# Turning half of the combination's low weights by DMA transposes, and splitting the low part of the slot embeddings

## The chip, the cores and the metric

The kernel runs on 1 core of a Trainium2 chip. The time is device microseconds (us) of one execution. Engines are named as in the profile: PE is TensorE (PEld its weight loads), DVE is VectorE, ACT is ScalarE, POOL is GpSimd, SP is SyncE, which here only issues DMAs. A name with a q (SPq, DVEq) is that engine's sequencer. A line number such as L2032 is a line of the kernel before.

## The reference, cut to what matters

A gated delta-rule attention layer, then a soft mixture of experts on its output. x is (4, 2048, 256) in float32.

```python
x = x + attn(layernorm(x))       # scan over 2048 tokens with a 128x128 state for each of 4 batches
xn = rms_norm(layernorm(x), gamma_x)
se = rms_norm(slot_embeds, gamma_slot)               # 8 x 128 = 1024 slots of 256
logits = einsum('bsd,etd->bset', xn, se)             # 2048 tokens x 1024 slots
dispatch = softmax(logits, axis=1)                   # over the tokens
slots = einsum('bsd,bset->betd', xn, dispatch)
processed = gelu(slots @ w1) @ w2                    # hidden width 1024
combine = softmax(logits over all slots, axis=-1)    # over the 1024 slots
x = x + einsum('bnd,bsn->bsd', processed, combine)   # the combination
```

## The kernel before

**The two parts.** `attention` works on chunks of 128 tokens of all four batches at once. Every engine runs the same software pipeline: `step(i, q)` for i from -4 to 15, in which an engine does its share for chunks i to i + 4. The order inside a step is written out by hand for each engine and the engines meet only through semaphores. `moe` then works through the four batches one after the other. A batch has logits and column maxima, dispatch (the slots' inputs), the expert layers (`hidden`, `processed`) for two halves of the slots, and at last the combination.

**High and low parts.** Products that need more than float16 are made of float16 pairs: a value's high part is its rounding to float16, its low part the rounded rest. A product then takes three matmuls: high by high, high by low, low by high.

**The combination.** A batch has 16 tiles of 128 tokens, written as (k, t) with k and t from 0 to 3. For each tile ACT takes the exponential of a row of L in place (`weights`, L1840, 128x1024). DVE casts it to the high part Wh (L1683) and subtracts to get the low part Wl (L1686), in `split_weights`. Both must be transposed, since the matmul contracts over the slots. Wh goes through a DMA transpose into Th that SP issues in `turn` (L1508). Wl is transposed on PE by eight 128x128 transposes into PSUM (`turn`, L2032), and ACT copies the result to Tl (`low_turned`, L1846). PE then makes 24 matmuls of 257 columns into PSUM (`combine`, L2047), and DVE divides by the last column and adds the residual (`finish`, L1745 and L1749). POOL issues the loads of the residual x1t (L1555) and the stores of the result (L1565).

PE's order in the combination is `turn(0,0)`, `processed(1)`, `turn(0,1)`, then for every tile `combine(k,t)` and `turn` of the tile two ahead. DVE's order is `finish(k,t)`, `split_weights(k+1,t)`. SP's order is `turn` tile by tile, in one queue. So each tile's weights are prepared four tiles before they are used, and there are four buffers of Wh, Wl and Th, but two of Tl and of the PSUM tile that the transposes write.

**The slots.** In `attention`, while the pipeline runs, the slot embeddings are scaled: DVE makes the row gxs = 16 gamma_x gamma_slot once (L707), and `slots_scaled` multiplies each of the 8 blocks of 128 slots by its norm's inverse and by gxs (L729), four blocks at each of two places of step -2. ACT makes the high part sp_h in step 0. `slots_low` makes the low part sp_l in one DVE instruction of 128x2048 (L736) in step 1, between the doubling n = 0 and `low_part`. PE transposes both in step 13 (`turn_slots`, which waits for `slots_ok` to be 3).

**DVE's step** in `attention` is, in order: 15 pairs of `product` (L611) and `column` (L622), which depend on each other one after the other, with other short work let in between at fixed counts s; `statistics_in` (L542), `residual` (L670), `moments_in` (L555), `decays` (L579), `system` (which writes M, L597), `doubling` 0 (L636), `low_part` (which writes Xl, L701), `statistics` (L680), `turned_low` (L563), `right_side` (L644), `doubling` 1 (L636), and the rest. PE's second `turn_Z` (L1169) and all that stands behind it in PE's order waits for doubling 0, its third for doubling 1.

## Time and profile before

| | |
|---|---|
| Time, median of 3 runs | 1182.07 us (1180.25 to 1182.2) |
| The profiled execution: its time | 1181.81 us |
| its span | 1180.2 us |
| mean granted clock of PE | 0.978 of full |
| PE busy | 1117.5 us, 95% |
| DVE busy | 944.2 us, 80% |
| ACT busy | 736.9 us, 62% |
| POOL busy | 322.9 us, 27% |
| DMA traffic | 93.97 MB, mean 80 GB/s |

The time is some 1.6 us longer than the span, which is what lies before the first and after the last instruction of the trace. A busy share is an average over stages with different limits, so what a change in one stage is worth has to be read from that stage.

### The profile page before, as it was taken

The page shows a single profiled execution, that of the slowest core. Times are in us where ns is not written, and L with a number is a line of the kernel's source. Part 1 is how long each engine was busy: PE and PEld are TensorE (multiplying, and loading weights), DVE is VectorE, ACT ScalarE, POOL GpSimd, SP SyncE. Part 2 cuts the span into 40 slices and gives each one's busy share as a digit, 9 for nine tenths or more (in the row PEclk, how much of TensorE's full clock was granted, in tenths as well). Part 3 has the DMA queues.
Part 4 walks back from the last instruction along what each step waited for, and adds up shares of the span by engine and source line. Part 5 has one row for each costly group of instructions (what it writes and reads, how often), then busy time and mean ns, then how long its engine had stood idle before and what let it go on. Part 6 is the DMA issues. An engine that isn't in the chain of part 4 may idle for free.

```text
span 1180.2 us, 26880 instructions
## 1 busy us (share of the span) xinstructions
PE 1117.5 (95%) x8600; PEld 860.1 (73%) x8600; DVE 944.2 (80%) x2193; ACT 736.9 (62%) x1386; POOL 322.9 (27%) x391
## 2 busy tenths in 40 slices
PE   4599899999999979999999999999999999999998
PEld 2487788888888765487786486787486787487787
DVE  5888888888888856998586998576998666998665
ACT  4446556666676545597663697674597764497763
POOL 3847555667556621000022000022000022000022
PEclk9699999999999988999999999999999999999999
DMA  6113322333323252331274031364030355000165
GB/s 198 49 45 99 117 78 83 89 89 114 109 80 89 82 129 67 99 73 45 63 157 95 2 72 36 72 137 114 2 72 27 72 129 129 1 2 1 19 125 126
DMA packets 185512, 93.97 MB, mean 80 GB/s; under 512 B 123680, under 2 KB 176928, under 8 KB 185440
## 3 DMA queue, kind: packets, MB, share of 16 engines
q1 hardware_dynamic: 178384, 75.40, 26.9%
q0 software_dynamic: 5792, 17.05, 5.0%
q8 instruction: 49, 0.80, 0.3%
q10 hardware_dynamic: 1264, 0.53, 0.2%
q14 instruction: 23, 0.19, 0.1%
HBM read 38.42 MB, written 29.36 MB: 57 GB/s over the span
## 4 chain that ended last, share of the span: by engine, by line
PE 71%; DVE 13%; issue 7%; ACT 3%; POOL 0%; DMA 0%; DVEq 0%; ACTq 0%; SPq 0%; POOLq 0%
PE m_wide L2047 14%; PE m_wide L1927 11%; PE m_wide L2021 7%; PE m_wide L2007 7%; PE a_bank L1118 4%; DVE m_Dm L1627 3%; PE a_bank L1130 3%; DVE m_El L1635 2%; PE m_wide L2032 2%; ACT m_Eh L1810 2%; PE a_bank L1180 2%; PE a_bank L1256 2%; PE a_bank L1169 2%; PE m_wide L1981 2%; PE a_bank L1220 1%
## 5 line engine op out<-in xcount | busy, mean ns | idle before, releaser
L1565 POOL DMA_DIRECT2D out_dram<-m_o x64 | 35.4, 553 | 620.9 <-DVE m_o L1749 508.9
L1981 PE MATMUL m_wide<-m_X,m_Eh 128*128 128x257 f16 (+1 forms) x1024 | 171.0, 273 | 2.1 <-DVE m_El L1635 1.6
L1927 PE MATMUL m_wide<-seT,XT 128*128 128x512 f16 x672 | 147.7, 380 | 1.0 <-issue 1.0
L2047 PE MATMUL m_wide<-m_Ph,m_Th 128*128 128x257 f16 x512 | 140.5, 274 | 0.0
L1981 PE MATMUL m_wide<-m_X,m_El 128*128 128x257 f16 (+1 forms) x512 | 139.8, 273 | 0.0
L2047 PE MATMUL m_wide<-m_Ph,m_Tl 128*128 128x257 f16 x512 | 139.5, 273 | 0.0
L2047 PE MATMUL m_wide<-m_Pl,m_Th 128*128 128x257 f16 x512 | 139.2, 272 | 0.0
L1927 PEld LDWEIGHTS m_wide<-seT,XT 128*128 (+1 forms) x672 | 65.7, 98 | 78.9 <-issue 2.0
L1981 PEld LDWEIGHTS m_wide<-m_X,m_Eh 128*128 128x128 f16 x1024 | 99.3, 98 | 18.9 <-issue 3.1
L1783 ACT COPY L<-m_wide 128x512 f32<-128x512 f32 (+1 forms) x112 | 65.1, 584 | 74.6 <-PE m_wide L1927 73.8
L1803 ACT ACTIVATE m_E<-m_Dm,m_eshift 128x512 f32<-128x512 f32 x128 | 92.5, 722 | 21.1 <-DVE m_Dm L1627 20.6
L1846 ACT COPY m_Tl<-m_wide 128x1024 f16<-128x1024 f16 x64 | 64.6, 1010 | 61.6 <-PE m_wide L2032 61.6
L1635 DVE TENSOR_TENSOR m_El<-m_E,m_Eh 128x512 f16<-128x512 f32 x128 | 87.8, 689 | 7.4 <-ACT m_Eh L1810 3.3
L1627 DVE TENSOR_TENSOR m_Dm<-L,m_Mb 128x512 f32<-128x512 f32 x128 | 87.7, 685 | 0.0
L2021 PE MATMUL m_wide<-w2s,m_hh 128*128 128x256 f16 x512 | 84.5, 273 | 0.0
L1598 DVE TENSOR_TENSOR cmax<-cmax,L 128x512 f32<-128x512 f32 x112 | 77.2, 689 | 8.0 <-ACT L L1783 6.6
L2007 PE MATMUL m_wide<-m_sTh,w1s 128*128 128x512 f16 x256 | 77.5, 379 | 0.0
L1810 ACT CAST m_Eh<-m_E 128x512 f16<-128x512 f32 x128 | 77.0, 604 | 0.0
L1604 DVE TENSOR_REDUCE rmax<-L 128x1 f32<-128x512 f32 (+1 forms) x112 | 76.1, 679 | 0.0
L1840 ACT ACTIVATE L<-L,m_nrm (+1 forms) x64 | 73.7, 1152 | 0.9 <-DVE m_nrm L1669 0.9
L2021 PE MATMUL m_wide<-w2s,m_hl 128*128 128x256 f16 x256 | 69.8, 273 | 0.0
L1660 DVE TENSOR_TENSOR m_hl<-m_E,m_hh 128x512 f16<-128x512 f32 x64 | 43.9, 692 | 24.6 <-ACT m_hh L1831 24.5
(199 smaller groups left out, 2739.9 us busy)
## 6 DMA issues: line engine op xcount, KB each, us to landing
L<-in_L_attn_x_dram SPq DMA_DIRECT2D x16, 512.0 KB, 6.8
Mrep<-M_dram SPq DMA_DIRECT2D x32, 256.0 KB
x_dram<-x SPq DMA_DIRECT2D x16, 512.0 KB, 6.3
m_X<-X_dram SPq DMA_DIRECT2D x128, 64.0 KB, 1.8
m_x1t<-x_dram POOLq DMA_DIRECT2D x32, 256.0 KB, 3.6
out_dram<-m_o POOLq DMA_DIRECT2D x64, 128.0 KB, 2.4
M_dram<-M_ SPq DMA_DIRECT2D x16, 256.0 KB, 2.6
X_dram<-Xh SPq DMA_DIRECT2D x16, 256.0 KB, 2.3
```

What stands on the lines that cost most here:

```text
L1598: dve.tensor_tensor(cmax[:, half_at], cmax[:, half_at], L[:, z, bass.ds(tile, 1), :] .rearrange("q a n -> q (a n)"), ALU.max).then_inc(cm_ ...
L1604: dve.tensor_reduce(rmax[:, bass.ds(z * NT + tile, 1)], L[:, z, bass.ds(tile, 1), :] .rearrange("q a n -> q (a n)"), AX.X, ALU.max, negate ...
L1627: dve.tensor_tensor(Dm[p][:, :], L[:, v, bass.ds(4 * g + t, 1), :] .rearrange("q a n -> q (a n)"), Mb[:, v * HS:(v + 1) * HS], ALU.subtrac ...
L1635: dve.tensor_tensor(El[t % 4][:, :], E[t % 4][:, :], Eh[t % 4][:, :], ALU.subtract)\
L1803: act.activation(E[t % 4][:, :], Dm[p][:, :], ACT.Exp, bias=eshift[:, 0:1]).then_inc(E_ok[p], 1)
L1810: act.copy(Eh[t % 4][:, :], E[t % 4][:, :]).then_inc(Eh_ok[p], 1)
L1840: act.activation(row, row, ACT.Exp, bias=nrm[:, bass.ds(4 * k + t, 1)]).then_inc(Ec_ok, 1)
L1927: last = pe.matmul(lg[t % 4], XT[:, sx * KD + k, bass.ds((4 * g + t) * P, P)], seT[:, ss, k, z * HS:(z + 1) * HS], start=(c == 0), stop=(c ...
L1981: last = pe.matmul(acc[v][q], e[t % 4][:, qs], X[:, sx, bass.ds(4 * g + t, 1), 0:XW].rearrange("q a n -> q (a n)"), start=first and e is E ...
L2007: last = pe.matmul(up[f % 2], w1s[:, sw, k, f * P:(f + 1) * P], sT[ss][:, k, :], start=(c == 0), stop=(c == 3 * KD - 1))
L2021: last = pe.matmul(down[q % 2], hT[sh][:, f, q * P:(q + 1) * P], w2s[:, sw, f, :], start=(c == 0), stop=(c == 3 * NF - 1))
L2047: last = pe.matmul(co[p], a, pp[:, e, 0:XW], start=(c == 0), stop=(c == 3 * NS - 1))
```

## The change

1. **Combination.** For tiles with odd t, the low part Wl is transposed by a DMA as well. SP's `turn` gets a second transpose of the same size right behind the first, into Tl_odd, which lies in the room of sTl (for t = 1) and sTh (for t = 3). Since these hold the slots' transposes that `hidden` reads, the first of them in a batch wait on SP for the first of `processed(1)`. PE's `turn` and ACT's `low_turned` are left out for odd t, and PE's and DVE's waits are changed to fit. PE's order is now `combine(k,0)`, `turn(k,2)`, `combine(k,1)`, `combine(k,2)`, `turn(k+1,0)`, `combine(k,3)`.
2. **Low part.** `slots_low` is cut into two instructions of half the size, and these stand between the `product` and `column` pairs, behind s = 3, the first in step 1 and the second in step 12.
3. **Scale row.** gxs is no longer in SBUF but in PSUM, in bank 2.

```diff
-        gxs = sb("gxs", [P, D])
+        gxs = bank[2][:, 0:D]
...
-            def slots_low():
+            def slots_low(first, past):
                 dve.wait_ge(slots_ok, 2)
-                dve.tensor_tensor(sp_l[:, :, :], slots_g[:, :, :], sp_h[:, :, :], ALU.subtract).then_inc(slots_ok, 1)
+                last = dve.tensor_tensor(sp_l[:, first:past, :], slots_g[:, first:past, :], sp_h[:, first:past, :],
+                                         ALU.subtract)
+                if past == NS:
+                    last.then_inc(slots_ok, 1)
...
+                    if s == 3:
+                        if at == 1:
+                            slots_low(0, NS // 2)
+                        if at == NCH - 4:
+                            slots_low(NS // 2, NS)
...
-                if at == 1:
-                    slots_low()
...
+        Tl_odd = [v[:, :, :].rearrange("q k n -> q (k n)").rearrange("q (e n) -> q e n", e=NS) for v in (sTl, sTh)]
...
                 sp.dma_start_transpose(Th[t][:, :, :], Wh[t]).then_inc(T_in[t], 16)
+                if t % 2 == 1:
+                    if isinstance(k, int):
+                        hidden_done = value(sp, (2 * b + 1) * (QS // 2) + 1)
+                        sp.wait_ge(pc, 1)
+                        sp.wait_ge(dn_ps[0], hidden_done)
+                        sp.sem_inc(turning, 1)
+                    sp.wait_ge(Wl_ok, m)
+                    sp.sem_inc(turning, 1)
+                    sp.dma_start_transpose(Tl_odd[t // 2], Wl[t][:, :]).then_inc(T_in[t], 16)
...
-                    dve.wait_ge(T_in[t], 16 * m)
+                    dve.wait_ge(T_in[t], 16 * m if t % 2 == 0 else 32 * m - 16)
...
-                    dve.wait_ge(tp_ps[t % 2], b * HB + 2 * k + t // 2 + 1)
+                    if t % 2 == 0:
+                        dve.wait_ge(tp_ps[t % 2], turned_before(b, k, t) + 2)
...
-                low_turned(0, 1)
                 with act.Fori(0, QB - 1) as k:
                     for t in range(4):
                         weights(k + 1, t)
-                        low_turned(k + (t + 2) // 4, (t + 2) % 4)
-                for t in range(2, 4):
-                    low_turned(QB - 1, t)
+                        if t % 2 == 0:
+                            low_turned(k + (t + 2) // 4, (t + 2) % 4)
+                low_turned(QB - 1, 2)
...
-                    pe.wait_ge(Tl_ok[p], n + 1)
-                    pe.wait_ge(T_in[t], 16 * (b * QB + k + 2))
+                    if t % 2 == 0:
+                        pe.wait_ge(Tl_ok[p], turned(b, k, t) + 1)
+                        pe.wait_ge(T_in[t], 16 * (b * QB + k + 2))
+                    else:
+                        pe.wait_ge(T_in[t], 32 * (b * QB + k) + 48)
...
-                        for a, pp in ((Th[t][:, e, :], Ph), (Th[t][:, e, :], Pl), (Tl[p][:, es], Ph)):
+                        for a, pp in ((Th[t][:, e, :], Ph), (Th[t][:, e, :], Pl),
+                                      (Tl[p][:, es] if t % 2 == 0 else Tl_odd[t // 2][:, e, :], Ph)):
...
                 processed(1)
-                turn(0, 1)
                 cut_to = value(pe, nb * QS + 1)
                 with pe.Fori(0, QB - 1) as k:
                     for t in range(4):
                         combine(k, t)
-                        turn(k + (t + 2) // 4, (t + 2) % 4)
+                        if t % 2 == 0:
+                            turn(k + (t + 2) // 4, (t + 2) % 4)
                 for t in range(4):
                     combine(QB - 1, t)
-                    if t < 2:
-                        turn(QB - 1, t + 2)
+                    if t == 0:
+                        turn(QB - 1, 2)
```

## Rows read from the trace of the kernel before

**Rows 1.** The chain that ended last, first batch's combination: start us, us, what

```profile
576.16 10.48 PE m_wide L2021 x96
586.64 0.45 PE m_wide L2032 x8
587.09 2.65 PE m_wide L2047 x24
...
630.46 5.30 PE m_wide L2047 x48
```

**Rows 2.** Groups by line: count | busy us, mean ns | idle before, releaser

```profile
L1846 ACT COPY m_Tl<-m_wide 128x1024 f16<-128x1024 f16 x64 | 64.6, 1010 | 61.6 <-PE m_wide L2032 61.6
L2032 PE MATMUL m_wide<-ident,m_Wl 128*128 128x128 f16 x512 | 39.0, 219 | 0.0
```

**Rows 3.** Timeline of DVE in the combination: start us, us, instruction

```profile
592.87 0.17 DVE L1745 RECIPROCAL m_cden<-m_wide 128x1 f32<-128x1 f32 x1
...
594.19 1.23 DVE L1686 TENSOR_TENSOR m_Wl<-L,m_Eh 128x1024 f16<-128x1024 f16 x1
```

**Rows 4.** The line that issues SP's transposes: ns min/median/max, and landing

```profile
L1508 SPq DMA_TRANSPOSE m_Th<-m_El x32: 1232/1238/1439, 580.3 to 1165.4; - x32
...
DMA to landing us min/median/max: 3.0/3.5/5.2
```

**Rows 5.** Timeline of SP's queue: the first two transposes of a batch

```profile
569.98 2.83 SPq L1508 DMA_TRANSPOSE m_Th<-m_Eh  x2
```

**Rows 6.** DMA queues in the combination, 590 to 630: packets, MB, engine share

```profile
q1 hardware_dynamic: 12672, 3.15, 50.9%
q0 software_dynamic: 1007, 3.01, 26.3%
```

**Rows 7.** Windows: length, busy PE PEld DVE ACT POOL (x count), PEclk, DMA share, GB/s

```profile
508.00:510.00 2.00, 2.00 (x21) 1.78 (x19) 1.91 (x4) 1.85 (x4) 0.00 (x0) 1.00 1.28 290
...
581.00:582.00 1.00, 1.00 (x11) 0.89 (x10) 0.75 (x2) 0.37 (x1) 0.00 (x0) 1.00 0.48 99
582.00:583.00 1.00, 1.00 (x12) 0.90 (x10) 0.96 (x3) 0.00 (x0) 0.00 (x0) 1.00 0.88 164
```

**Rows 8.** Timeline of DVE's system (M), one each step of attention

```profile
133.93 0.69 DVE L597 TENSOR_TENSOR M_<-a_bank,gamb_ 128x512 f32<-128x512 f32 x1 [0.64 <-DVE gamb_ L579]
...
165.17 0.69 DVE L597 TENSOR_TENSOR M_<-a_bank,gamb_ 128x512 f32<-128x512 f32 x1 [0.66 <-PE a_bank L1160]
...
214.04 0.69 DVE L597 TENSOR_TENSOR M_<-a_bank,gamb_ 128x512 f32<-128x512 f32 x1 [0.59 <-PE a_bank L1160]
...
358.56 0.69 DVE L597 TENSOR_TENSOR M_<-a_bank,gamb_ 128x512 f32<-128x512 f32 x1 [0.61 <-PE a_bank L1160]
```

**Rows 9.** Timeline of step 1, where the low part stands now

```profile
136.14 2.44 DVE L736 TENSOR_TENSOR L<-L 128x2048 f16<-128x2048 f32 x1
...
138.51 2.28 DVE L701 TENSOR_TENSOR Xl<-xf,Xh 128x1024 f16<-128x1024 f32 x1
...
143.02 1.12 PE L1169 MATMUL a_bank<-a_const,Z_ 128*128 128x128 f32 x4 [3.08 <-DVE Z_ L636]
```

**Rows 10.** Windows of step 1, columns as in rows 7

```profile
145.00:147.00 2.00, 2.00 (x13) 1.36 (x12) 0.43 (x1) 0.40 (x2) 0.00 (x0) 0.50 0.67 232
```

**Rows 11.** Timeline of step 1's columns: a bias on DVE, then PE's queries

```profile
123.35 0.42 DVE L570 SCALAR_TENSOR_TENSOR L<-a_bank,bkv 128x258 f32<-128x258 f32 x1
...
124.17 0.38 PE L1130 MATMUL a_bank<-L,wqg_h 128*128 128x512 f16 x1
```

**Rows 12.** Timeline of step -2 and the scaled slots' line: ns min/median/max

```profile
59.29 0.41 DVE L636 TENSOR_TENSOR Z_<-Z_,a_bank 128x256 f32<-128x256 f32 x1
...
63.97 1.05 PE L1193 MATMUL a_bank<-Z_,P1T 128*128 128x64 f32 x8
...
66.06 0.41 DVE L636 TENSOR_TENSOR Z_<-Z_,a_bank 128x256 f32<-128x256 f32 x1
...
L729 DVE SCALAR_TENSOR_TENSOR L<-XT,srn,gxs x8: 454/1476/1744, 55.4 to 63.5; 128x256 f32<-128x256 f32 x8
```

More of the change, by code:

```diff
@@ L1481, in moe, with turned, turned_before @@
         T_in = [sem(f"T_in{u}") for u in range(4)]
+        def turned(b, k, t):
+            return b * HB + 2 * k + t // 2 + 1
+        def turned_before(b, k, t):
+            return turned(b, k, t) - 2
         @block.sync
@@ L1843, in low_turned @@
                     p, n = t % 2, b * HB + 2 * k + t // 2 + 1
-                    act.wait_ge(tp_ps[p], n + 2)
+                    act.wait_ge(tp_ps[p], turned(b, k, t) + 2)
                     act.wait_ge(co_ps[p], n + 1)
@@ L1965, in batch @@
                         for p in range(2):
-                            pe.wait_ge(Tl_ok[p], HB * b + 1)
+                            if p == 0:
+                                pe.wait_ge(Tl_ok[p], HB * b + 1)
                         turn_maxima(0)
@@ L2026, in turn @@
                 def turn(k, t):
-                    p, n = t % 2, b * HB + 2 * k + t // 2 + 1
+                    p = t % 2
                     pe.wait_ge(Wl_ok, b * NT + 4 * k + t + 1)
-                    pe.wait_ge(Tl_ok[p], n)
+                    pe.wait_ge(Tl_ok[p], turned(b, k, t))
                     for e in range(NS):
```

## The prediction

> **What bounds the kernel now.** I read the shares first: PE is busy 95% of the span, but that is a mean over stages, so I went on to the chain that ended last, stage by stage. In the combination it is PE alone: eight transposes (0.45 us), 24 matmuls (2.65 us), again and again with nothing between [rows 1]. A tile costs 3.10 us, and no other engine's time shows. So there a piece of PE's work taken away shortens the kernel by its whole length, until something else becomes the slowest. In attention PE and DVE take turns on the chain. I measured that stage by the distance between two instructions of one kind, one a step [rows 8]: from 214.04 to 358.56 are six steps of 24.09 us, but the one from 133.93 to 165.17 took 31.24. The reader is to see two things: a stage with one bound, and one step of sixteen that is 7.15 us longer than its like. The change touches both.
>
> **The transposes taken from PE.** Of 16 `turn` in a batch 8 go, 32 in the kernel, each 0.45 us on the chain [rows 1]: 14.4 us less. Rows 2 bear out the count: 512 transposes, eight for each of 64 tiles. With them go 32 of ACT's copies of 1.01 us [rows 2], which cost nothing now, as ACT sat waiting for PE before them, and give nothing. The mean tile is then 2.65 + 0.45/2 = 2.875 us, four tiles 11.5.
>
> **Does DVE keep up?** From a tile's reciprocal to the end of its low part are 2.55 us when they run back to back (592.87 to 595.42) [rows 3], below 2.875. The new wait of DVE for the second transpose is for a buffer used four tiles before. No cost, but the cover shrinks from 0.55 to 0.33 us a tile.
>
> **Does SP keep up?** A transpose takes SP 1.24 us [rows 4], and two in a row 2.83 with the waits between [rows 5], so 1.6 us each. Three for each two tiles are 4.8 of 5.75 us. It fits. Behind the new wait for Wl on SP stands the next tile's transpose of Wh. After `combine(k,t)` ends, DVE has Wh some 1.7 us and Wl some 3.1 us later. Wh's landing, 3.5 us from issue [rows 4], has room. For an odd tile: ready at 3.1, landed at 6.6 to 6.8, needed when `combine(k+1,t)` starts, which is 11.5 - 2.65 = 8.85 us after. That leaves about 2 us of slack. At a batch's start the first Tl_odd waits for the first quarter of `processed(1)`, which runs from 576.16 in four equal parts [rows 1], so till 578.8. It lands about 582.4, and the second combination starts after 589: hidden. The wait holds up SP's transpose for tile 2, whose Wh comes later than that anyway.
>
> **Do the DMA engines keep up?** This is the doubtful term. In the combination q1 (the transposes) holds them 50.9% of 40 us for 3.15 MB, which is 12.0 tiles of 0.262 MB, so 1.70 us each; q0 (x1t and results) 26.3%, which over 12.9 tiles is 0.81 us a tile [rows 6]. The new need is 1.5 x 1.70 + 0.81 = 3.36 us a tile, more than 2.875. But a transpose alone takes 0.48 + 0.88 = 1.36 [rows 7], since under load the packets of the two queues stretch each other, and then the need is 1.5 x 1.36 + 0.81 = 2.85. And the share is no hard ceiling at 1: it stood at 1.28 in a window of XT's transposes [rows 7], by which 3.36 would need only 2.63 us. Bounds of the cost: below nothing, as the need is 2.63 to 2.85; above, (3.36 - 2.875) x 12 tiles (the first four of a batch are turned before it starts) = 5.8 us less the 2 us of slack, 3.8 a batch, 15 in all. A gain is excluded. I take 1.5 us in all, near the low end, since two of the three readings lie under 2.875.
>
> By the Trainium skill (DMA: Bandwidth & Descriptors, Issuing engines are not separate DMA queues) DMAs issued from different engines run on the same 16 engines and interleave, which speaks against this change: SP's third transpose takes its time from POOL's loads and stores. The stretch from 1.36 to 1.70 agrees. The same page (Latency and other measured facts) gives 261 GB/s for a transposing DMA in an unfavourable layout; by that 0.262 MB would take an estimated 1.0 us and the need would be 2.3, no stall at all. The trace has 1.36, and goes first.
>
> **The low part leaves its place in step 1.** There one instruction of 2.44 us stands ahead of `low_part`, and that takes 2.28 [rows 9]. PE's third `turn_Z` sits idle 3.08 us for DVE [rows 9], and then PE runs at a granted clock of 0.50, the 1.2 GHz level, at 145 to 147 [rows 10]. So step 1 pays three times: the instruction, the stretched `low_part` behind it, and slow matmuls. With it gone the step should be like its neighbours: 7.15 us less. The two steps after it, (214.04 - 165.17)/2 = 24.44 each [rows 8], should also come to 24.09: 0.7 less. Bounds: 2.44, if the clock falls anyway, to 7.85.
>
> **Its halves in the columns.** Each is half the size, 1.22 us, in a chain that DVE runs without gaps. Behind it on DVE stand two biases; PE's queries wait for the second. That ended at 123.77 and they started at 124.17 [rows 11], so a shift of 1.22 delays PE by 0.8. DVE's own end of step has about 0.64 us of idle time before M [rows 8], so it needs no more. Two halves (step 12 is alike): 1.6 us more, bounds 0 and 2.4. The clock is safe here: PE is in dense matmuls at the time, and a gap of 0.8 is far from 3.08. `turn_slots` in step 13 finds the second half done a step before.
>
> **The scale row in PSUM.** The eight scalings took 1476 ns in the median, but one took 454 [rows 12], so most were held up and not working. In the second group of four the doubling waits behind them: it began at 66.06, and PE's product for it was there at 63.97 + 1.05 = 65.02 [rows 12], so 1.04 us are lost there. For the first group, whose doubling came at 59.29, I add 0.6 as an estimate: PE's other work hides the rest. 1.7 us less. Bounds: nothing, if they stay held up, and 8 x (1.476 - 0.454) = 8.2, if all of it counted; the rows at the doubling are nearer.
>
> By the Trainium skill (SBUF — State Buffer, the section on the shared port pair) a DVE instruction with two SBUF inputs and a GpSimd one that reads SBUF take one port pair in turns, each for its whole length. By that rule a PSUM row ends the hold-up, and the scalings fall to about 0.45 each; without it they stay at 1.48 and this term is 0. The row's spread of 454 to 1744 ns agrees with the rule, which names the cause that I assume.
>
> **Sum.** -14.4 + 1.5 - 7.15 - 0.7 + 1.6 - 1.7 = -20.85. The profiled execution took 1181.81, so 1161.0. The median of the runs is 0.3 higher, so the new median may be too; I say 1161.
>
> **The rivals.**
> 1. The DMA engines become the bound of the combination. For it: the need of 3.36 by the loaded rows. Against: the other two readings, and that a batch's stage is only 12 tiles long with 2 us of slack. It gives between 1163 and 1161 - 1.5 + 15 = 1174.5; half the price is 1167.
> 2. The clock or the stretch stays in attention: the halves open a new gap, or step 1 gives back its 2.44 us alone. Then 7.85 - 2.44 = 5.4 us are missing: 1166.4. For it: PE's other stalls in steps 12 to 15. Against: only step 1 shows the low clock.
> 3. Slower than before, by one loop: the landing of the second transpose. A tile's loop is combine 2.65, DVE 3.1, then the time L from Wl to landing; it must fit in four tiles. Without stalls the sum is -22.35; spread over 48 looped tiles that is 0.47 each, so the kernel is slower once a tile takes over 3.34, that is once L is over 4 x 3.34 - 5.75 = 7.6 us. With L = 8: 3.44 a tile, +27, so 1186.5. For it: the transpose queues behind that of Wh, and four other transfers. Against: landing is 3.5 in the median and at most 5.2 [rows 4].
> 4. The change does little in attention but works in the combination, because the steps' excess has another cause: 1161 + 7.85 + 1.7 = 1170.5. The idle time in rows 9 speaks against it.
>
> **Chances.** Forecast (1158 to 1164) 0.60; rival 1 0.18; rival 2 0.11; rival 4 0.05; rival 3 0.04; within 0.2% of before, by a loaded queue whose price just eats the gain, 0.02. From 1157 to 1173 all but rival 3, that sliver and the far end of rival 1 are held. 0.2%, 2.4 us, is about what a measurement of this kernel can tell from no change. So faster 0.94, same 0.02, slower 0.04.
>
> **What would show it.** In the combination's chain: 2.65 twice for each 0.45, and no wait of PE before L2047; if rival 1 holds, L2047 waits for a DMA, and the first tiles of a batch are clean while later ones are not. The landing of L1508 should rise above 3.5 but stay under 5.5. M in step 1: about 25 us after the one before, granted clock 1.00 throughout; step 12 about 0.8 longer than now. The scalings at about 0.45 us. What would make me wrong: a new stall of PE in `combine`, a low clock in any step, or a DVE that no longer catches up because results land late.

## The result and the profile after

The kernel with the change takes 1162.84 us in the median of four runs (1161.44 to 1165.45), the kernel before 1181.49 beside it. The ratio is 0.9846, with an interval of 0.9826 to 0.9866: 18.7 us faster, where 20.9 were forecast. A second set of five runs on another chip gave 1162.43 against 1182.72, ratio 0.9832 (0.9819 to 0.9845), which is 20.3 us. The execution that was profiled first took 1165.45 (span 1163.8), the slowest of its four. A second profile was taken in the second set, of an execution of 1162.43. The first has the larger stalls, and both are read below.

The page of the kernel after: the busy shares, and from the costliest groups the combination's matmuls and ACT's copies.

```profile
PE 1098.5 (94%) x8344; PEld 841.1 (72%) x8344; DVE 936.2 (80%) x2194; ACT 705.2 (61%) x1354; POOL 321.5 (28%) x391
...
L2076 PE MATMUL m_wide<-m_Ph,m_Th 128*128 128x257 f16 x512 | 141.3, 276 | 6.1 <-DMA m_sTh<-m_Wl 6.0
...
L1871 ACT COPY m_Tl<-m_wide 128x1024 f16<-128x1024 f16 x32 | 32.4, 1013 | 69.7 <-PE m_wide L2057 69.7
```

PE's busy time fell by 19.0 us, from 1117.5 to 1098.5, which is more than the 14.4 of the 32 turns; the rest is in the main matmuls that no longer run at half clock in step 1, where PE is busy 23.8 us instead of 27.9. The copies are 32 instead of the 64 of [rows 2]. The group of `combine` (L2047 before, L2076 now) has a new kind of idle time: 6.0 us, ended by the DMA that writes m_sTh from Wl. It is the only new wait of PE.

**The combination.** The chain of the first batch, to be laid beside [rows 1]:

```profile
575.97 2.65 PE m_wide L2076 x24
578.62 0.45 PE m_wide L2057 x8
579.06 5.30 PE m_wide L2076 x48
...
607.36 0.45 PE m_wide L2057 x8
607.81 2.67 PE m_wide L2076 x24
...
611.88 1.24 SPq L1523
...
613.23 6.30 DMA m_sTh<-m_Wl
...
619.58 2.82 PE m_wide L2076 x24
622.41 17.70 PE m_wide L1951 x82
```

Two tiles, one turn, again and again: 5.75 us for two tiles, as forecast. At the batch's end the chain leaves PE and passes through DVE and SP to a transpose of Wl that took 6.30 us to land. From the first matmul of `processed(1)` (565.49) to the logits of the next batch (622.41) are 56.92 us. Before, the same distance was 59.60 to 59.63 in each of the four batches. The eight turns that went take 3.56 of that (8 x 0.445, the length of a turn in the chain), which would leave 56.04. So the batch stalled for 0.88 us. The four batches took 56.92, 61.27, 57.73 and 57.28, 233.2 in all instead of 238.4: 14.3 us of work are gone, and 9.1 came back as stalls. In the second profile they took 56.98, 56.77, 56.85 and 56.95, 227.6 in all, with 3.4 us of stalls. The worst batch of the first profile, in its chain:

```profile
783.65 1.28 SPq L1523
...
785.08 1.89 SPq L1532
...
787.42 2.61 SPq L1523
...
790.36 1.25 SPq L1523
...
791.73 7.94 DMA m_sTh<-m_Wl
...
799.72 4.48 PE m_wide L2076 x24
804.20 20.72 PE m_wide L1951 x96
```

Three things are longer here than they were before: SP needs 2.61 and 1.89 us to issue a transpose that took it 1.24 in the kernel before [rows 4], the landing takes 7.94 us, and the tile behind the wait takes 4.48 instead of 2.65. SP's queue is part of this path: from 783.65 on it issues one after the other, with no wait for data between. The tile before the last one in the loop of its buffer ended at 788.0, and the last low part was issued 3.7 us after that, where it was 2.76 in the first batch. So of the stall some 1 us came from SP's queue and 1.6 from the longer landing; 0.7 were there in the first batch already. The only wait of PE in the middle of a batch, at 967 in the third, looks alike: there SP took 2.82 us for one issue. Windows of the same place:

```profile
797.00:800.00 3.00, 0.28 (x3) 0.26 (x4) 0.47 (x1) 0.00 (x0) 0.00 (x0) 1.00 0.33 57
800.00:804.00 4.00, 4.00 (x24) 2.92 (x22) 0.01 (x1) 0.00 (x0) 0.54 (x1) 0.57 0.09 33
```

PE sat idle for 3.26 us, and then its granted clock was 0.57 in the mean over 4 us, so some 3.4 of them were at the 1.2 GHz level. The stall of 3.3 us cost 5.2.

**Attention.** The timeline of DVE's M, one a step, with the low part's first half and two of `low_part`, to be laid beside [rows 8, 9]. Step 1 is counted from its M at 131.43 to the next:

```profile
106.71 0.69 DVE L597 TENSOR_TENSOR M_<-a_bank,gamb_ 128x512 f32<-128x512 f32 x1 [1.88 <-issue]
...
118.33 1.22 DVE L736 TENSOR_TENSOR L<-L 128x1024 f16<-128x1024 f32 x1
131.43 0.69 DVE L597 TENSOR_TENSOR M_<-a_bank,gamb_ 128x512 f32<-128x512 f32 x1 [0.60 <-DVE gamb_ L579]
...
133.65 1.42 DVE L701 TENSOR_TENSOR Xl<-xf,Xh 128x1024 f16<-128x1024 f32 x1
...
155.55 0.69 DVE L597 TENSOR_TENSOR M_<-a_bank,gamb_ 128x512 f32<-128x512 f32 x1 [0.67 <-PE a_bank L1166]
...
157.76 2.29 DVE L701 TENSOR_TENSOR Xl<-xf,Xh 128x1024 f16<-128x1024 f32 x1
```

Step 1 takes 155.55 - 131.43 = 24.12 us instead of 31.24, and the granted clock is 1.00 in every window of it. The step before it holds the half in its columns: 24.72 where it took 23.81. The other steps are what they were: 24.64 for the next, then 23.98. Step 12 grew by 0.93. The step that scales the slots fell from 30.12 to 27.3 (28.06 in the second profile). These four differences add up to -7.12 + 0.91 + 0.93 - 2.8 = -8.1 us. The scalings in the timeline of step -2:

```profile
54.84 1.62 DVE L729 SCALAR_TENSOR_TENSOR L<-XT,srn,a_bank 128x256 f32<-128x256 f32 x4
57.74 1.63 DVE L729 SCALAR_TENSOR_TENSOR L<-XT,srn,a_bank 128x256 f32<-128x256 f32 x4
```

Four take 1.62 us. A single one takes 0.47 in the median, where [rows 12] had 1.48.

### The profile page after: what moved, and what is told of

The parts are those of the page before. It is cut to its first block, busy times and chain, and to the rows that moved or that the text cites. A ratio compares the mean times of both kernels' runs of the same rounds, so it can differ in the third digit from the quotient of the medians.

```text
span 1163.8 us, 26301 instructions
## 1 busy us (share of the span) xinstructions
PE 1098.5 (94%) x8344; PEld 841.1 (72%) x8344; DVE 936.2 (80%) x2194; ACT 705.2 (61%) x1354; POOL 321.5 (28%) x391
## 4 chain that ended last, share of the span: by engine, by line
PE 70%; DVE 10%; issue 8%; DMA 4%; ACT 3%; POOL 3%; SPq 2%; DVEq 0%; POOLq 0%; ACTq 0%
PE m_wide L1951 11%; PE m_wide L2076 10%; PE m_wide L2046 7%; PE m_wide L2032 7%; PE m_wide L2006 5%; PE a_bank L1124 4%; PE a_bank L1136 3%; PE a_bank L1186 3%; DMA m_sTh<-m_Wl 3%; DVE m_Dm L1651 2%; PE a_bank L1175 2%; PE a_bank L1262 2%; DVE m_El L1659 2%; ACT m_Eh L1835 2%; PE a_bank L1199 2%
## 5 line engine op out<-in xcount | busy, mean ns | idle before, releaser
L2076 PE MATMUL m_wide<-m_Ph,m_Th 128*128 128x257 f16 x512 | 141.3, 276 | 6.1 <-DMA m_sTh<-m_Wl 6.0
L2076 PE MATMUL m_wide<-m_Pl,m_Th 128*128 128x257 f16 x512 | 139.9, 273 | 0.0
L2006 PEld LDWEIGHTS m_wide<-m_X,m_Eh 128*128 128x128 f16 x1024 | 99.4, 98 | 18.7 <-issue 3.5
L1871 ACT COPY m_Tl<-m_wide 128x1024 f16<-128x1024 f16 x32 | 32.4, 1013 | 69.7 <-PE m_wide L2057 69.7
L1865 ACT ACTIVATE L<-L,m_nrm (+1 forms) x64 | 71.3, 1146 | 0.9 <-DVE m_nrm L1693 0.9
L2076 PE MATMUL m_wide<-m_Ph,m_Tl 128*128 128x257 f16 x256 | 69.7, 272 | 0.0
```

Source lines behind the costliest of these rows:

```text
L1865: act.activation(row, row, ACT.Exp, bias=nrm[:, bass.ds(4 * k + t, 1)]).then_inc(Ec_ok, 1)
L2006: last = pe.matmul(acc[v][q], e[t % 4][:, qs], X[:, sx, bass.ds(4 * g + t, 1), 0:XW].rearrange("q a n -> q (a n)"), start=first and e is E ...
L2076: last = pe.matmul(co[p], a, pp[:, e, 0:XW], start=(c == 0), stop=(c == 3 * NS - 1))
```

## The experiments

Where nothing else is said, a diff is against the kernel with the change.

### Each half of the change alone

The combination alone puts the scale row and `slots_low` back:

```diff
-        gxs = bank[2][:, 0:D]
+        gxs = sb("gxs", [P, D])
...
-                        if at == 1:
-                            slots_low(0, NS // 2)
-                        if at == NCH - 4:
-                            slots_low(NS // 2, NS)
...
+                if at == 1:
+                    slots_low()
```

> The combination part alone, attention as before. Theory A (the 14.4 us of transposes are saved, but in each batch the landing of the last odd tiles is late because the 16 DMA engines are full; some 6 us are lost again): 8 us less than before, 1173.5. Rival B (the two parts need each other, so that the combination alone gives little): under 4 us less, above 1177.5. If the loss were a trait of the profiled run alone: 14 us less, 1167.5.

Measured: 1172.16 against 1182.73, ratio 0.9914 (0.99 to 0.9927), 10.6 us faster. That lies between the 8 of theory A and the 14 of a change without stalls. The four batches took 56.89, 56.88, 57.76 and 56.28: 3.7 us of stalls, where theory A had 6.

This run shows one thing more. Its low part stands in the old place, as it does in the kernel before and in the kernel with the scale row alone. PE's idle time in step 1 is the same in the three profiles, 3.08 to 3.09 us, but what follows differs. Here:

```profile
144.68 1.12 PE L1169 MATMUL a_bank<-a_const,Z_ 128*128 128x128 f32 x4 [3.08 <-DVE Z_ L636]
...
147.00:149.00 2.00, 2.00 (x18) 1.60 (x18) 0.49 (x2) 0.37 (x1) 0.00 (x0) 0.73 0.61 209
```

In the kernel before the clock stays low for longer:

```profile
149.00:151.00 2.00, 2.00 (x11) 1.70 (x10) 1.69 (x8) 0.00 (x0) 0.88 (x3) 0.50 0.00 0
```

Windows of half a microsecond give 3.4 us at the low level here, 6.8 with the scale row alone and 10.2 before, and step 1 takes 28.63, 30.06 and 31.24 us. So each 3.4 us of low clock lengthen the step by 1.2 to 1.4. Carried on to no low clock at all, that is some 27.3 us, an estimate.

Attention alone, as its diff against the kernel before:

```diff
-        gxs = sb("gxs", [P, D])
+        gxs = bank[2][:, 0:D]
...
-            def slots_low():
+            def slots_low(first, past):
...
+                        if at == 1:
+                            slots_low(0, NS // 2)
+                        if at == NCH - 4:
+                            slots_low(NS // 2, NS)
...
-                if at == 1:
-                    slots_low()
```

> The low part in halves and the scale row in PSUM alone, combination as before. Theory A (step 1 loses its 7.1 us, the scalings 2.8, the halves cost 0.9 each, the rest of attention follows): 10 us less, 1171.5. Rival B (the gain before the combination is partly chance of the profiled run): 6 us less, 1175.5. With e1 the two should add up to the whole change, 18.65.

Measured: 1173.2 against 1182.73, ratio 0.9922 (0.9908 to 0.9935), 9.5 us faster. Theory A had said 10. The steps are those of the whole change (24.12 for step 1), and the batches' stages are 59.6 again. The parts add up to 20.1 us, as the whole does in its second set (20.3): within the scatter the two halves don't touch each other.

### Is it the number of transposes?

Only tiles with t = 1 have their low part turned by DMA. Tiles with t = 3 go back to PE. The rest of the diff fits waits and counts to it.

```diff
...
-                if t % 2 == 1:
+                if t == 1:
...
-                        if t % 2 == 0:
+                        if (t + 2) % 4 != 1:
                             turn(k + (t + 2) // 4, (t + 2) % 4)
...
```

> The change, but only tiles with t = 1 go by the DMA transpose, those with t = 3 are turned on PE again. Theory A (DMA engines): the need falls to between 1.25 x 1.36 + 0.81 = 2.5 and 1.25 x 1.70 + 0.81 = 2.9 us a tile, against a tile of 2.99, so no stall: of the 14.4 us 7.2 are left and nothing is lost again, so 1181.5 - 7.2 - 10.5 = 1163.8, about the same as the full change. Rival B (any second transpose in a row makes tiles late): a stall of 2 to 3 us, 1166 or more. Landing of the transposes at most 5.5 us by A.

Measured: 1166.52 against 1182.73, ratio 0.9869 (0.9854 to 0.9884), 16.2 us faster. The stages are 57.81, three times, and 57.85, 231.3 in all. That is 7.1 under the kernel before, what the 16 turns take (16 x 0.445), with no stall. By its total alone the run would have spoken for the rival (1166 or more). But theory A's 1163.8 had counted 10.5 us for attention, which alone gave 9.5, and a kernel before of 1181.5, which was 1182.73 here; 1182.73 - 7.1 - 9.5 = 1166.1. The low parts landed in 4.6 us in the median and 5.5 at most, as A had said. The end of its first batch, in the chain:

```profile
616.74 0.45 PE m_wide L2059 x8
617.19 2.65 PE m_wide L2078 x24
619.84 0.45 PE m_wide L2059 x8
620.28 5.30 PE m_wide L2078 x48
625.59 14.46 PE m_wide L1954 x67
```

So five transposes for four tiles come in time, and six don't quite. The second step down, from t = 1 to t = 1 and 3, brought 3.7 us of its 7 by the medians and the second profile; in the first profile, with 9.1 us of stalls, the stages were 1.9 longer than here.

### POOL's transfers, or SP's queue?

A late transpose can be late because POOL's loads and stores take the DMA engines, or because SP's queue has three to issue. This kernel leaves SP's queue as it is, with all its transposes, and lets POOL's transfers move 16 rows instead of 128 or 256, so most of the output is not written.

```diff
...
-                pool.dma_start(x1t[u][:, :, :], x1_dram[bass.ds(b, 1), bass.ds(at, 2 * P), :]
-                               .rearrange("b (p q) d -> q (b p) d", p=2)).then_inc(x1_in[u], 16)
+                pool.dma_start(x1t[u][0:16, 0, :], x1_dram[bass.ds(b, 1), bass.ds(at, 16), :]
+                               .rearrange("b q d -> (b q) d")).then_inc(x1_in[u], 16)
...
-                               .rearrange("b q d -> (b q) d"), o[p][:, :]).then_inc(o_out[p], 16)
+                               .rearrange("b q d -> (b q) d"), o[p][0:16, :]).then_inc(o_out[p], 16)
```

> The change, but in the combination the residual's loads and the results' stores move only 16 rows of 128 (a sixteenth to an eighth of the bytes), so most of the output is not written and half of the residual not read. SP's queue and all waits are as they are. Theory A (the DMA engines are shared between the transposes and these transfers): no stall, PE never waits for a transpose in the combination, landing at most 4.5 us, 1156.5, six under the change. Rival B (SP's own queue, three transposes for each two tiles in order, is what makes them late): the stalls stay, 1162.

The stages are 56.03, 56.02, 56.03 and 56.06: every stall is gone. The landing of the low transposes, first in the kernel with the change, then here:

```profile
L1532 SPq DMA_TRANSPOSE m_sTl<-m_Wl x16: 1232/1610/2822, 568.3 to 1144.5; - x16
...
DMA to landing us min/median/max: 3.0/5.0/7.9
```

```profile
L1532 SPq DMA_TRANSPOSE m_sTl<-m_Wl x16: 1232/1292/1858, 573.9 to 1142.7; - x16
...
DMA to landing us min/median/max: 3.1/3.4/4.8
```

Three transposes for two tiles are no load that SP can't issue or that the DMA engines can't carry. What makes them late are POOL's transfers. The longest landing, 4.8 us, is a little over the 4.5 expected. That the lateness comes from the engines that both use, and not from the memory behind them, this run doesn't separate; for it speak the shares of the two queues, which add up to more than 1 (below).

The time of this kernel missed the 1156.5 expected of it by 11 us: 1167.92 (ratio 0.9872, 0.9857 to 0.9887). Two causes are seen in its trace, and neither lies in the combination. The stage between attention and the first batch's experts was 171.3 us long, against 167.2 and 168.4 in the two profiles of the kernel with the change, and behind the landing of the last store lie some 7 us in which the trace shows nothing:

```profile
1156.92 0.48 DVE L1776 SCALAR_TENSOR_TENSOR m_o<-m_wide,m_cden,m_x1t 128x256 f32<-128x256 f32 x1
1158.12 0.49 POOL L1591 DMA_DIRECT2D out_dram<-m_o  x1 [2.25 <-DVE m_o L1776]
```

The span is 1167.1, and the store landed 1.7 us after its issue. What the last 7 us are stays open. The stages answer the question of this experiment, the total doesn't.

### The last tile of a batch

In the second profile of the change PE waits once in each batch, for 0.6 to 0.8 us, and each time at the last tile, (3, 3). In the first profile four of five waits stand there. If that one alone is too tight, turning it on PE should take the stall away for one turn a batch. Waits and counts are again fitted to it.

```diff
...
-                if t % 2 == 1:
+                if t % 2 == 1 and not (last and t == 3):
...
-                    if t == 0:
-                        turn(QB - 1, 2)
+                    if t < 2:
+                        turn(QB - 1, t + 2)
...
```

> The change, but the last tile of each batch is turned on PE again. Theory A (the backlog of the DMA engines grows through a batch and is paid at its last tile): four times 0.45 us more for PE, and the stall at the last tile goes, so each combination takes 56.04 + 0.45 = 56.5; 3 us less than the change. Rival B (the stall only moves to the odd tile before, or to the stores): no gain, or 1 to 2 us more.

Measured: 1159.88 against 1182.72, ratio 0.9812 (0.9799 to 0.9825), 22.8 us faster. The kernel with the change had 1162.43 on the same chip. The stages are 56.47, 56.47, 57.31 and 56.5; the work without stalls is 56.04 + 0.445 = 56.48. Three batches have no stall, and the third waited once, for an odd tile with t = 1. The sum of the stages, 226.75, is 0.8 below that of the second profile of the change, which is what this edit is shown to bring; the other 1.7 of the difference of the medians are not in the combination. In the profiles 0.9 us lie ahead of the first one, which the edit doesn't touch, so they are most likely scatter.

### Was it the size of the low part or its place?

The halves go back to the place where the whole stood, one in step 1 and one in step 12.

```diff
-                    if s == 3:
-                        if at == 1:
-                            slots_low(0, NS // 2)
-                        if at == NCH - 4:
-                            slots_low(NS // 2, NS)
...
+                if at == 1:
+                    slots_low(0, NS // 2)
+                if at == NCH - 4:
+                    slots_low(NS // 2, NS)
```

> The change, but the two halves of the low part stand behind the doublings, where the whole stood before, in steps 1 and 12, and no longer in the columns. Theory A (step 1 was long in three parts: the instruction, low_part held up behind it, and PE's clock, which fell after an idle time of 3.08 us): with 1.22 instead of 2.44 us PE's idle time is 1.9 us or less and the clock stays at 1.00, so step 1 takes 24.1 + 1.2 to 2.3, 25.3 to 26.4, and the time is within 2 us of the change. Rival B (any added work at this place costs the clock): step 1 takes 28 or more, a granted clock of 0.50 is seen, and the time is 4 us over the change.

Measured: 1166.84 against 1182.72 in seven runs, ratio 0.9851 (0.9838 to 0.9864), so 4.4 us slower than the change. Theory A, under which the clock would stay up, was wrong: step 1 takes 30.16 us. The timeline of it, and windows behind:

```profile
134.21 1.38 DVE L736 TENSOR_TENSOR L<-L 128x1024 f16<-128x1024 f32 x1
...
135.51 2.28 DVE L701 TENSOR_TENSOR Xl<-xf,Xh 128x1024 f16<-128x1024 f32 x1
...
136.66 2.25 POOL L438 TENSOR_TENSOR kTg_<-kT,gbc_ 128x512 f32<-128x512 f32 x1
...
140.03 1.12 PE L1174 MATMUL a_bank<-a_const,Z_ 128*128 128x128 f32 x4 [2.02 <-DVE Z_ L636]
```

```profile
135.00:140.00 5.00, 2.90 (x24) 2.45 (x24) 5.00 (x8) 1.37 (x3) 5.00 (x3) 0.95 0.44 138
140.00:142.00 2.00, 1.97 (x9) 1.61 (x10) 1.91 (x8) 0.82 (x2) 1.92 (x3) 0.50 1.03 326
142.00:145.00 3.00, 3.00 (x19) 1.85 (x17) 0.51 (x2) 0.41 (x2) 0.00 (x0) 0.50 0.51 169
```

PE was idle for 2.02 us here instead of 3.08, and its clock fell all the same, to 0.50 until 150. So at this place even half the size brings the stall and the low clock. Half the instruction saved 1.1 us of the step and no more: the low clock lasted 10.2 us here too, so this is like against like with the kernel before. To see whether the clock falls in each execution, the same kernel was profiled again.

> A second profile of the halves at the old place, whose runs lay between 1164.6 and 1172.2 us. Theory A (after an idle time of PE of some 2 us the clock falls in some executions and not in others): this time step 1 may be about 26.4 us at a granted clock of 1.00, with the time near 1165, or again 30.2 with 0.50 and a time over 1167; the idle time is 2.0 us in both. Rival B (the clock has nothing to do with the spread): step 1 is 30.2 at 0.50 again while the time is near 1165.

It took 1167.62. Step 1 was 30.38 us, the idle time of PE 2.02 again, and the clock 0.50 at 142 to 150. So in both profiles the clock was low. Their difference of 4.5 us lies elsewhere: the batches' stages add up to 231.0 us in the first, with 6.8 of stalls, and to 227.3 in the second, with 3.1. But neither is one of the three executions of 1164.6 to 1164.9. Those have a mean granted clock of 0.982 to 0.984, and the other four of the seven, from 1166.8 up, 0.978 to 0.981. Whether step 1 ran at full clock in them, no trace shows.

### A place that costs nothing?

The two halves in the columns cost 1.8 us together. Here the whole low part stands in step 13, behind s = 8 (the text below says 7), where DVE was seen idle.

```diff
-                        if at == 1:
-                            slots_low(0, NS // 2)
-                        if at == NCH - 4:
-                            slots_low(NS // 2, NS)
...
+                        if at == NCH - 3:
+                            slots_low(0, NS)
```

> The change, but the low part is one instruction of 2.44 us again, in the columns of step 13, behind s = 7, where DVE sits idle for PE's scores for 2.4 us in the kernel before. Theory A (the halves cost 0.9 us each in steps 1 and 12 since nothing hides them; here it is hidden): 1.8 us less than the change. Rival B (step 13 is bound by what follows the columns on DVE): no gain, or a loss of up to 2.4.

Measured: 1161.62 against 1182.72, ratio 0.9823 (0.981 to 0.9836). The 1.8 us are gone from the steps (23.81 where the first half stood, 24.45 where the second did), yet the last M comes only 1.0 earlier, at 398.55 for 399.52, since the steps up to the scalings were 0.9 longer in this execution. The total is 0.8 less, within the scatter, where 1.8 were expected.

### The scale row alone

The kernel before with one line changed:

```diff
-        gxs = sb("gxs", [P, D])
+        gxs = bank[2][:, 0:D]
```

> The kernel before with only the scale row moved to PSUM. Theory A (the scalings were held up by POOL's instructions, and a row in PSUM ends that): eight scalings at about 0.41 us instead of 1.48, step -1 to 0 (M to M) 27.3 instead of 30.1, step 1 stays at 31.2, time 2.8 less than before. Rival B (the scalings take their time whatever else runs): no change.

Measured, with 11 runs against 15: 1179.88 against 1182.14, ratio 0.9982 (0.9972 to 0.9992), 2.3 us faster, where 2.8 were expected. The step of the scalings fell from 30.12 to 26.99. Step 1, with the old low part, took 30.06 and not 31.24: that is its shorter stretch of low clock, told of above. The scalings:

```profile
58.55 1.63 DVE L729 SCALAR_TENSOR_TENSOR L<-XT,srn,a_bank 128x256 f32<-128x256 f32 x4
60.47 0.42 DVE L636 TENSOR_TENSOR Z_<-Z_,a_bank 128x256 f32<-128x256 f32 x1 [0.29 <-PE a_bank L1193]
...
61.46 1.63 DVE L729 SCALAR_TENSOR_TENSOR L<-XT,srn,a_bank 128x256 f32<-128x256 f32 x4
```

The doubling between the two groups now waits 0.29 us for PE's product, so the scalings ahead of it no longer make it late. Before, that doubling began at 59.29 [rows 12], 5.10 us after the step's M; now it begins 3.16 us after it, so it had lost 1.94. The doubling behind the second group now waits for PE too (0.88 us); from one doubling to the other are 5.58 us instead of 6.77, so it had lost another 1.19, of which 1.04 were read in [rows 12]. The two add up to the 3.13 of the step.

The kernel before also shows what the scalings waited for. Five of the eight took 1.48 to 1.74 us, and each of the five ended 0.3 us after an instruction of POOL did. The three that took 0.45 to 0.47 began while POOL was idle, between 58.29 and 60.49. With the row in PSUM all eight take 0.45 to 0.48, beside POOL's instructions too.

### The best of both

The last tile on PE and the low part in step 13 together.

> The change with both amendments: the last tile of a batch turned on PE, and the low part whole in step 13 where DVE is idle. Theory A (they touch different stages): each combination 56.5, no halves in steps 1 and 12, the sum of both gains, 2.5 + 0.8 to 1.8 us less than the change, so a ratio to before of 0.980. Rival B (e7's gain was mostly chance, as its combinations were only 0.8 us shorter in sum): 0.982.

Measured: 1161.16 against 1182.14, ratio 0.9827 (0.9812 to 0.9841). The last M came at 396.82 and the stages are 56.69, 56.47, 57.16 and 56.5, so both edits do in the trace what they did alone; in the time no gain over either can be told. The ratio expected was 0.980 if both gains were real, and 0.982 if most of the last tile's was chance. It fits the second. The kernel with the change once more, on the chip of the last tile's experiment:

> The changed kernel itself, on the chip of the next three, for comparison with them. The length of the four combinations (from the start of the second processed to the next logits) is 59.60 before and 56.04 without any stall. Theory A (stalls come and go with the phase of the transfers): some 57.2 each, 5 us over in the sum of four. If the stall of 5.2 in one batch of the first profile were the rule: 9 us over again.

That is the second set of runs told of above. Its stalls were 3.4 us, where theory A had 5, and the 9 of the first profile did not come again.

## Why the prediction was right, point by point

- **The total.** 1161.0 was forecast, and 1162.84 and 1162.43 measured. The two sides of the sum were off in opposite directions: the combination by 2.3 us (-12.9 forecast, -10.6 alone), attention by 1.5 (-7.95 forecast, -9.5 alone). That the total came out so near is in part luck. And the result lies where the forecast's range overlaps the low end of rival 1 (1163); the execution profiled first, with 1165.45, lies beyond the forecast's 1164.
- **The transposes taken from PE.** Right: 14.3 us of work went, and with one in four by DMA just its 7.1.
- **DVE and ACT keep up.** Right. PE's chain shows no wait for either of them. The low part of the last tile was issued 2.76 us after `combine` of the tile before it in the loop had ended (610.47 to 613.23), where 3.1 was assumed.
- **The DMA engines.** The term of 1.5 us was mis-sized: 3.4 us in the second profile of the change, 3.7 with the combination alone, 9.1 in the first profile. The mechanism is the one that rival 1 names, with its sign (clean tiles first, a wait later). Its half price was 6 us more than forecast; 2 more were found in two of the profiles, and 7.6 in the first. Of the three readings of the need, the loaded one was right. In the first batch's combination the queues show:

```profile
q1 hardware_dynamic: 17936, 4.45, 75.8%
q0 software_dynamic: 1072, 3.15, 32.7%
```

  This is of the window 585 to 620. 4.45 MB are 17.0 transposes, those of 11.3 tiles; the shares add up to 1.085 of 35 us, so 3.36 us a tile, as [rows 6] had given. The sum is the same by chance: a transpose takes 1.56 instead of 1.70, and POOL's part 1.01 a tile instead of 0.81. But the share was no ceiling: 3.36 in 2.875 us needs a share of 1.17, and in the fourth batch it stood there for 15 us, at 227 GB/s:

```profile
1130.00:1145.00 15.00, 14.92 (x148) 13.10 (x147) 12.55 (x21) 6.87 (x8) 4.92 (x8) 1.00 1.18 227
```

  So the engines carried the load at PE's pace, and the transposes landed late. The statement that the landing would stay under 5.5 us failed: 5.0 in the median and up to 7.9. POOL's stores landed later too, 3.4 us in the median and 7.2 at most instead of 2.4 and 4.0, and DVE waited for them (3.6 us in the second batch), but PE was not held up by that.
- **The slack.** This is the step that was too wide. Between two tiles with the same t lie four tiles less one, 8.85 us, but for the batch's last tile one turn fewer stands between (611 to 619 in the chain above): 8.4. Its loop of 2.76 + 6.30 us is 9.06, so it is late by 0.7, and with a landing of 5.5 it would not be. Odd tiles inside a batch have 0.45 more; in the second profile none of them made PE wait, in the first one did. By the Trainium skill (DMA: Bandwidth & Descriptors, Issuing engines are not separate DMA queues), DMAs of SP and POOL interleave on the same 16 engines; the trace agrees, as a landing of 5.0 us became 3.4 in the median when POOL's transfers shrank.
- **The clock in the combination.** It was taken to be safe, as no stall was counted behind which it could fall. In the worst batch it fell after 3.26 us of idle time and added 1.8.
- **The low part leaves step 1.** -7.15 forecast, -7.12 measured, and so close only because both come from the same execution before: with the low part in the same place step 1 took 31.24, 30.06 and 28.63 us in three profiles. Of the three costs that step 1 was said to pay, these give the weights: by the estimate of 27.3 us without the low clock, the slow matmuls were worth some 4 of the 7.1, and the instruction, the stretched `low_part` and the stall some 3, of which 1.1 are half of the instruction. `low_part` took 1.42 us in step 1 after the change; but it takes 2.29 in step 2 with no low part ahead of it, so the place behind the low part isn't all that stretches it.
- **The two steps after it.** -0.7 forecast, nothing measured: 24.64 as before. These steps have another cause, which no run tested. The excess is in the first of them, and there `low_part` takes 2.3 us instead of 1.2 to 1.3 (at 157.76 above), before and after alike. It does so in step 11 too, beside the same instruction of POOL (L438).
- **The halves.** +1.6 forecast, +0.91 and +0.93 measured.
- **The scale row.** -1.7 forecast. -2.8 in the trace of the change, -3.1 in that of the row alone, and 2.3 in its time. The instruction fell to 0.47 us. The term was too small at the first group's doubling: 0.6 was added there as an estimate, and it had lost 1.94. Most of the time there was taken to be hidden, and wasn't. By the Trainium skill (SBUF — State Buffer, Who interferes with whom) a DVE instruction with at most one SBUF input, outside its modes that use both ports, doesn't contend with GpSimd. The trace agrees: 1.48 us became 0.47 with nothing changed but the place of one operand.
- **The rivals.** Rival 2 has no row for it: the clock is 1.00 through steps 0 and 1. Rival 3 needed landings over 7.6 us in every tile; the longest of 32 was 7.9. Rival 4 fell with step 1.

What stays open: why the stalls differ from one execution to the next with the same order of transfers (3.1 to 9.1 us in six profiles), why the low clock in step 1 lasts 3.4, 6.8 or 10.2 us after the same idle time, and some 2 us between the end of attention and the first combination (10.7 saved by the second half of the first batch's experts, 8.7 by the last M), where the length of the stage (166.9 to 171.3 us over all profiles, changed or not) and the granted clock differ from one execution to the next (0.89 in the mean from 400 to 480 before, 0.94 and 0.91 in the two profiles after).

## What to carry to other kernels

When work is moved from the bound engine to the DMAs, don't ask only whether their mean share has room: write down the loop from the producer to the landing for each tile, the last one of a batch too, and compare it with the landing under the new load and not with that of before. A long instruction costs what it stops: the same subtraction cost some 4 to 7 us ahead of a chain that fed PE, and 1.8 us in a place where PE had other work. And where an instruction's duration varies threefold for one shape, look who shares its operands' memory before its work is counted.

## What the runs showed of the hardware

- The share of the 16 DMA engines that the profile gives isn't bounded by 1: transposes beside POOL's copies ran at 1.18 for 15 us, and the transfers still landed, up to 7.9 us after their issue.
- A loaded queue shows up in the issuing engine: SP's 1.24 us for a transpose became 1.6 in the median and 2.8 at most for those of Wl. With POOL's transfers small it was 1.3 and 2.4.
- An idle time of PE of 2.02 us in step 1 was followed by a granted clock of 0.50 for about 10 us, in both profiles of that kernel. One of 3.08 us at the same place was followed by 3.4, 6.8 and 10.2 us in three profiles, so the idle time alone doesn't set how long the clock stays low. After 3.26 us in the combination it was low for some 3.4 us.
- A GpSimd instruction of 128x512 (L438) took 1.27 us in the median of its 16 and 2.25 in step 1 beside DVE's subtraction with two SBUF inputs, while that took 2.28 for 1.22: both were longer in one stretch. In the kernel with the change this pair is as long in steps 2 and 11, and not in step 1.
- A DVE instruction of 128x256 with two SBUF inputs took 0.45 to 0.47 us while POOL was idle, and 1.48 to 1.74 beside POOL's, ending 0.3 us after one of them each time. With one input in PSUM it took 0.45 to 0.48 either way.
